# Tower of embedding, attention and product-key feed-forward on one core: key weights multiplied behind the embedding, and layer norm, scores and top-k of the product-key stage begun in the tail of the first attention

## The chip, the cores and the metric

One core of one Trainium2 chip runs the whole program. The metric is the device time of one execution in microseconds (us), lower is better. The core has a matrix engine (TensorE, PE in the profile; its weight loads are PEld), VectorE (DVE), ScalarE (ACT), GpSimd (POOL) and SyncE (SP), which here only issues DMA transfers. Each engine executes its own list of instructions in order, and the lists meet at semaphores.

## The reference

What is computed, cut to the stages (z is layer-normalised h; B = 4 sequences, S = 512 tokens, D = 128):

```python
h = event_table[x] + value_table[itok] + mask * (tanh(num * w1 + b1) @ w2 + b2)
h = h + attention0(layernorm(h))          # 8 heads of 16, distance-corrected logits
# product-key feed-forward on z = layernorm(h):
q = (z @ Wq + bq).reshape(-1, 8, 128)     # 8 heads
s1 = einsum('bhc,hnc->bhn', q[..., :64], keys[:, 0])   # 64 scores
s2 = einsum('bhc,hnc->bhn', q[..., 64:], keys[:, 1])   # 64 scores
s1t, i1 = top_k(s1, 8);  s2t, i2 = top_k(s2, 8)
scores, best = top_k(s1t[..., :, None] + s2t[..., None, :], 8)
idx = i1 * 64 + i2 at best
vals = relu(z . w_down[idx]) * softmax(scores)
h = h + vals @ w_up[idx]
h = h + attention1(layernorm(h))          # 8 heads of 64
h = h + experts(layernorm(h))             # 16 experts, top-k tokens per expert
```

## The kernel before

The residual stream `h` stays in on-chip memory for the whole program as 16 tiles of 128 tokens; a batch is one sequence of 4 tiles. The stages follow each other, and each engine's part is written out by hand in one function per engine (`sync`, `gpsimd`, `scalar`, `vector`, `tensor`), so the order of the work is the order of the lines.

**Start.** SyncE issues 16 small and middle loads. GpSimd issues 32 indirect gathers of table rows (L346), eight per batch: batches 0 and 1, then the reciprocal root of the first layer norm (`rstd_step`, L356), then batches 2 and 3, then a power for the first attention (L374). TensorE makes the numeric part of the embedding of all four batches (L1141), VectorE adds it up (`embed`), makes the statistics of batch 0 (`ln_stats`, L689 to L694) and normalises (`ln_scale`, L701). `heads0` then makes queries, keys and values.

**First attention.** `attention(a0, b)` runs 32 units (8 heads x 4 tiles) through all engines: logits on TensorE, maximum on VectorE (L717), exponential on ScalarE (L463), division on GpSimd (L364), transposition on TensorE (L1097), split copies on ScalarE (L472) and VectorE (`expT_lo`, L730), product with the values on TensorE (`pv`, L1109), which runs eight steps behind the logits. For batches 0 to 2 the call is given `next_ln`: VectorE puts the statistics of the next batch behind unit 28's `expT_lo` (s == UNITS) and the scaling behind unit 30's, and TensorE transposes the result at s == UNITS + 3. For batch 3 nothing is given. `project0` (L1132, L1133) waits for the copy of the last product (L477) and writes bank 6; `residual` (L747) adds it to `h`.

**Product keys.** After that residual SyncE loads `pk_wqT` and `pk_keys` (512 KB each) into `vals_t`; VectorE spreads the bias (L853); TensorE folds query weights and keys into one matrix, `keyw`, and the bias into `keyb` (L1198, four groups of four products, each product two passes); ScalarE and VectorE copy them out (L534, L538, L946). Then come `ln_stats(lnC, 0)` on VectorE, `rstd_step` and `normalise_xn(0)` (L423) on GpSimd. From there tile t goes: `scores(t)` on TensorE (transpose L1210, products L1218 and L1219, the latter with `ones_r` and `keyb`), copy to `sc` on ScalarE (L548), `half_max` (L858), `half_index` (L865), `pair_scores` (L870), `pair_best` (L876 to L883) and `expert_numbers` (from L890) on VectorE, `expert_numbers` on GpSimd (L401 to L414), `transpose_uvp` on TensorE (L1226), then `one_hots` on VectorE (from L918) and `spread`. `expert_numbers` on VectorE waits at L893 for the exponential of the pair scores. ScalarE makes that exponential (`softmax_exp(0)`, L572) behind `copy_scores(1)`, the eight pieces of `relu_inner(0)` (L557) and `expand_indices(0)` (L566), and TensorE makes the products for those eight pieces (`inner(0)`, L1237) behind `scores(1)`. Tiles 0 and 1 are prepared in this way ahead of the loop over the 16 tiles; in the loop tile t + 2 is prepared beside tile t. TensorE's list at this place is:

```python
scores(0, 0)
scores(1, 0)
inner(0, 1)
transpose_uvp(0)
scores(2, 1)
transpose_uvp(1)
for t in range(NT):
    spread(t, 0, 2)
```

After the 16 tiles come the second attention and the experts, which the change doesn't touch.

Of the kernel before, what the change touches and what calls it, by code (L numbers as in the profile page):

```python
# [13 lines left out]
def tower(nc, x_idx, val_idx, num_rows, mask_idx, event_table, value_table, tok_w1, tok_b1, tok_w2b2,  # L14
# [7 lines left out]
    P = 128  # L22
# [5 lines left out]
    H = 8  # L28
# [19 lines left out]
    LOGITS = (0, 1, 6)  # L48
    GATED = 9

    with ExitStack() as ctx:
# [38 lines left out]
        wo0 = sb("wo0", [P, H // HPG, D])  # L90
        wqkv0 = sb("wqkv0", [P, 3 * D])
# [53 lines left out]
        k4 = qkv0[:, :, D:2 * D].rearrange("p j (h d) -> p j h d", h=H)  # L145
        qa = q_aug[:].rearrange("p (j h) a -> p j h a", j=TPB)
# [10 lines left out]
        w_v = sC.sb("w_v", [P, T2, 2, 2, NV, 2], F16)  # L157
        iota_u = sC.sb("iota_u", [P, NU, 2], F16)
        iota8 = sC.sb("iota8", [P, TOP, HK], F16)
        ident16 = sC.sb("ident16", [P, P], F16)  # L160
        wqT_s = vals_t[:, 0:1024].rearrange("p (h d) -> p h d", h=H)
        keys_s = vals_t[:, 1024:2048].rearrange("p (h n) -> p h n", h=H)
        bqb_s = vals_t[:, 2048:3072].rearrange("p (h t) -> p h t", h=H)
        keyw = sC.sb("keyw", [P, H * P])
        keyb = sC.sb("keyb", [P, H * P], F32R)
        ones_r = sC.sb("ones_r", [P, P], F32R)
# [4 lines left out]
        g_sb = sC.sb("g_sb", [P, 3, GT * NV])  # L171
# [120 lines left out]
        def _(sp):  # L292
# [15 lines left out]
            sp.dma_start(wo0[:], a0_wo.rearrange("p (g d) -> p g d", g=H // HPG)).then_inc(ld_a0, 16)  # L308
            sp.wait_ge(h_ready, B)
# [23 lines left out]
        def _(pool):  # L333
            nc.gpsimd.memset(ident[:], 0.0)
            nc.gpsimd.memset(ones[:], 1.0)
            nc.gpsimd.memset(mhalf[:], -0.5)
            nc.gpsimd.memset(phalf[:], 0.5)
# [44 lines left out]
            pool.wait_ge(a0.add, B)  # L382
# [5 lines left out]
            nc.gpsimd.memset(psp[:], 0.0)  # L388
            nc.gpsimd.memset(ones_r[:].bitcast(F32), 1.0).then_inc(consts, 1)
# [37 lines left out]
            rstd_step(lnC, 0, TPB)  # L427
            normalise_xn(0)
# [19 lines left out]
        def _(act):  # L448
# [5 lines left out]
            def attention(a, b, next_ln=None):  # L454
# [24 lines left out]
                for s in range(UNITS + 9):  # L479
# [7 lines left out]
                    if s == UNITS + 4 and next_ln is not None:  # L487
                        copy_xnT(next_ln, b + 1)

# [33 lines left out]

            copy_xnT(lnB, 0)
# [4 lines left out]
            attention(a0, B - 1)  # L529


            for n in range(2):
                act.wait_ge(kw_ps, n + 1)
                nc.scalar.copy(keyw[:, n * 512:(n + 1) * 512], bank[n][:, :]).then_inc(kw_sb, 1)  # L534
# [915 lines left out]
```

## Time and profile before

| | before |
|---|---|
| median of 3 runs | 1363.96 us (1362.43 to 1366.89) |
| the profiled execution | 1364.92 us, its span 1363.1 us |
| busy share of the span | PE 80%, PEld 61%, DVE 76%, ACT 51%, POOL 47% |
| granted TensorE clock over the span | 0.919 of full |
| DMA over the span | 14.63 MB, 11 GB/s on average |

The profile shows one execution; the span begins with its first instruction and ends with its last, and 1.82 us of its time lie outside. A share is an average over stages with different limits, so the stage around the change is read by itself below. "L1198" is line 1198 of the kernel before.

### The profile page before, as it was taken

The numbers are of one execution on the slowest core, as the hardware profiler recorded it, in microseconds if no ns is written. First come the engines' busy times: TensorE is split into PE (matmuls) and PEld (weight loads), VectorE is DVE, ScalarE is ACT, GpSimd is POOL, SyncE is SP. The second block draws the span as 40 slices with busy tenths as digits, with TensorE's granted clock in tenths as the row PEclk, the third lists the DMA queues.
The fourth block names the chain that finished last, engine by engine and source line by source line (L and its number), as shares of the span: only waits on it lengthen the run. The fifth ranks groups of instructions, "written<-read, shape, count | busy, mean of one in ns | idle before, by whom it ended". The sixth has DMA issues, their size and how long they took to land.

```text
span 1363.1 us, 24162 instructions
## 1 busy us (share of the span) xinstructions
PE 1091.6 (80%) x7848; PEld 835.8 (61%) x7848; DVE 1032.9 (76%) x2991; ACT 689.3 (51%) x1457; POOL 643.4 (47%) x530
## 2 busy tenths in 40 slices
PE   4386785867943888888888878789999898979997
PEld 2354554545532777777777778455665655656675
DVE  4697685976828999999999997387585876844587
ACT  1484674856713344344434433277484775815433
POOL 7474361743623776876677665154260542610000
PEclk9698897998977899898899989899899899978999
DMA  3300000000000000000000001100000000000000
GB/s 78 142 1 1 0 0 0 0 0 0 1 31 1 1 2 2 2 2 2 1 2 2 1 2 40 77 1 1 0 0 0 0 0 1 1 1 1 1 8 23
DMA packets 6425, 14.63 MB, mean 11 GB/s; under 512 B 1855, under 2 KB 4482, under 8 KB 5762
## 3 DMA queue, kind: packets, MB, share of 16 engines
q1 hardware_dynamic: 5314, 11.42, 2.4%
q0 software_dynamic: 1024, 2.10, 0.6%
q8 instruction: 49, 0.80, 0.3%
q14 instruction: 38, 0.31, 0.1%
HBM read 12.47 MB, written 1.05 MB: 10 GB/s over the span
## 4 chain that ended last, share of the span: by engine, by line
issue 32%; DVE 31%; PE 25%; POOL 6%; DVEq 3%; ACT 2%; POOLq 1%; DMA 0%; ACTq 0%; SPq 0%
DVE one_u L927 6%; DVE w_v L921 5%; PE quad L1349 4%; PE quad L1097 4%; PE bank L1344 4%; DVE a_eT L730 4%; DVE i L865 3%; PE quad L1109 3%; POOL wu L346 2%; DVE vals L936 2%; DVE m L858 2%; DVE bi L883 2%; POOL a_en L364 1%; DVEq L920 1%; DVE a_negmax L717 1%
## 5 line engine op out<-in xcount | busy, mean ns | idle before, releaser
L364 POOL TENSOR_TENSOR a_en<-a_e,a_rrec 128x512 f32<-128x512 f32 x256 | 265.1, 1040 | 300.7 <-DVE a_rrec L724 282.9
L717 DVE TENSOR_REDUCE a_negmax<-bank 128x1 f32<-128x512 f32 x256 | 176.1, 691 | 44.7 <-PE bank L1295 28.3
L463 ACT ACTIVATE a_e<-bank,a_negmax 128x512 f32<-128x512 f32 x256 | 176.3, 689 | 64.2 <-DVE a_negmax L717 53.6
L1097 PE MATMUL quad<-ident,a_en 128*128 128x128 f32 x1024 | 166.4, 287 | 42.1 <-DVE a_eT L730 35.2
L1097 PEld LDWEIGHTS quad<-ident,a_en 128*128 128x128 f32 x1024 | 112.4, 145 | 135.4 <-issue 121.7
L730 DVE TENSOR_TENSOR a_eT<-quad,a_eT 128x512 fp32r<-128x512 f32 x256 | 172.6, 676 | 4.5 <-ACT a_eT L472 4.3
L1109 PE MATMUL quad<-a_eT,a_v 128*128 128x512 f32 x512 | 174.1, 431 | 1.0 <-DVE a_eT L730 0.9
L396 POOL TENSOR_TENSOR vals<-relu_in,g_sb 128x512 f32<-128x512 f32 x80 | 141.3, 1792 | 40.4 <-ACT g_sb L590 21.3
L472 ACT CAST a_eT<-quad 128x512 fp32r<-128x512 f32 x256 | 148.0, 578 | 15.2 <-PE quad L1097 15.2
L1237 PE MATMUL bank<-xnT,wd 128*128 128x128 f32 x1024 | 129.0, 283 | 3.1 <-ACT relu_in L557 1.3
L1237 PEld LDWEIGHTS bank<-xnT,wd 128*128 128x128 f32 x1024 | 121.5, 195 | 8.8 <-ACT relu_in L557 8.4
L1268 PE MATMUL bank<-wu,vals 128*128 128x128 f32 x1024 | 119.3, 278 | 4.8 <-issue 4.8
L1268 PEld LDWEIGHTS bank<-wu,vals 128*128 128x128 f32 x1024 | 117.9, 195 | 4.9 <-issue 4.9
L1257 PE MATMUL quad<-w_v,one_u 128*128 128x64 f16 x2048 | 77.6, 199 | 46.5 <-DVE one_u L927 25.4
L1257 PEld LDWEIGHTS quad<-w_v,one_u 128*128 128x128 f16 x2048 | 71.0, 101 | 59.9 <-DVE one_u L927 35.0
L927 DVE TENSOR_TENSOR one_u<-iota_u,uv 128x2048 f16<-128x2048 f16 x64 | 97.4, 1580 | 0.0
L1295 PE MATMUL bank<-a_kT,a_qT 128*128 128x512 f32 x256 | 84.8, 419 | 9.3 <-DVE a_v L998 6.9
L557 ACT ACTIVATE relu_in<-bank 128x512 f32<-128x512 f32 x128 | 75.2, 596 | 24.1 <-PE bank L1237 22.4
L1349 PEld LDWEIGHTS quad<-wu,hidT 128*128 128x128 f32 x512 | 67.6, 194 | 31.4 <-issue 27.4
L1109 PEld LDWEIGHTS quad<-a_eT,a_v 128*128 128x128 f32 x512 | 79.6, 190 | 5.9 <-DVE a_eT L730 2.4
L590 ACT COPY g_sb<-quad 128x512 f32<-128x512 f32 x16 | 9.4, 587 | 138.9 <-PE quad L1257 138.9
L661 ACT ACTIVATE hidT<-bank,b1e 128x512 f32<-128x512 f32 x64 | 44.0, 687 | 62.7 <-PE bank L1344 62.4
(210 smaller groups left out, 2023.2 us busy)
## 6 DMA issues: line engine op xcount, KB each, us to landing
wd<-in_pk_down SPq DMA_DIRECT2D x1, 2048.0 KB, 8.3
wu<-in_pk_up SPq DMA_DIRECT2D x1, 2048.0 KB, 12.8
wu<-in_moe_w SPq DMA_DIRECT2D x2, 1024.0 KB
out<-h SPq DMA_DIRECT2D x4, 256.0 KB, 2.3
wd<-in_num_rows SPq DMA_DIRECT2D x1, 512.0 KB
vals<-in_pk_wqT SPq DMA_DIRECT2D x1, 512.0 KB, 3.7
vals<-in_pk_keys SPq DMA_DIRECT2D x1, 512.0 KB, 4.6
wd<-in_a_wq SPq DMA_DIRECT2D x1, 512.0 KB
```

The source lines that it names most:

```text
L364: nc.gpsimd.tensor_tensor(m.en[:, s % 3, :], m.e[:, s % 3, :], m.rrec[:, s % 4:s % 4 + 1].to_broadcast([P, S]), ALU.mult).then_inc(a.nr, 1)
L396: nc.gpsimd.tensor_tensor(*weigh_args(t, c, k, g_sb[:, slot, :])).then_inc(vals_pool, 1)
L463: nc.scalar.activation(m.e[:, s % 3, :], bank[LOGITS[s % 3]][:, :], ACT.Exp, bias=m.negmax[:, s % 4:s % 4 + 1], accum_out=m.rowsum[:, s % ...
L472: nc.scalar.copy(m.eT[:, hd % 2, 0, :, j * P:(j + 1) * P], bank[2 + s % 2].rearrange("p (c n) -> p c n", c=TPB)).then_inc(a.hi, 1)
L717: V.tensor_reduce(m.negmax[:, s % 4:s % 4 + 1], bank[LOGITS[s % 3]][:, :], AX.X, ALU.max, negate=True).then_inc(a.mx, 1)
L730: V.tensor_tensor(part[:, 1], bank[2 + s % 2].rearrange("p (c n) -> p c n", c=TPB), part[:, 0].bitcast(F32), ALU.subtract).then_inc(a.lo, 1)
L927: V.tensor_tensor(one_u[:, c * n:(c + 1) * n], iota_u[:].unsqueeze(1).to_broadcast([P, n, NU, 2]), token_pairs(uv[:, t % 2, 0, c * GT:(c + ...
L1097: last = tp(bank[2 + s % 2][:, c * P:(c + 1) * P], m.en[:, s % 3, c * P:(c + 1) * P], ident[:])
L1109: last = mm(bank[4 + g % 2], m.v[:, c, hd, :], m.eT[:, hd % 2, part, c, :], start=(hd % a.group == 0 and c == 0 and part == 0), stop=(hd % ...
L1237: last = mm(bank[g % 2][:, q * P:(q + 1) * P], wd[:, IG * g + q, :], xnT_tile(t), start=True, stop=True)
L1257: made = mm(quad[:, 2 * (c % 2) + i // half_pair, cols], one_u[:, pair // 2, :, pair % 2], w_v[:, pair // 2, k, :, :, pair % 2].rearrange( ...
L1268: last = mm(bank[6][:, 0:D], vals[:, v, :], wu[:, v, :], start=(v == 0), stop=(v == NV - 1))
```

## The change

The key weights are loaded, multiplied and copied in the start of the program, and the first tile of the product-key stage is normalised, scored and searched in the tail of the last batch's attention. In detail:

- SyncE: the loads of `pk_wqT` and `pk_keys` stand directly behind the load of `wo0` and go to the memory of `q_st`, which the first attention uses later. Before they waited for the last residual of the attention.
- `keyw`, `keyb` and `ones_r` get memory of their own; `ones_r` is filled in GpSimd's first instructions, `keyb` cleared in VectorE's first.
- TensorE multiplies the key weights behind the embedding products, into banks 1, 2, 3 and 7 (`KEY_BANKS`); it waits for the copies before it transposes the first normalised batch. ScalarE copies them before `copy_xnT(lnB, 0)`, VectorE does its part between `ln_stats` and `ln_scale` of batch 0.
- The last `attention(a0, B - 1)` is given `lnC` on VectorE, for batch 0 (tiles 0 to 3), and a `tail` on TensorE (transpose of tile 0 at s == UNITS + 3, its score products at UNITS + 5, ahead of the last two `pv` steps) and on ScalarE (copies at UNITS + 4 and UNITS + 6, ahead of the last `outT`).
- GpSimd no longer normalises batch 0 (`normalise_xn(0)` goes; VectorE does it) and makes its constants right behind `rstd_step(lnC, 0)`, without waiting for the residual.
- VectorE's residual of batch 3 moves behind the top-k search of tile 0, ahead of `expert_numbers(0)`. `scores(1)` and `inner(0)` stay behind `project0` on TensorE.
- `g_sb` and a placeholder `attention_tail` are laid out so that what the tail writes doesn't lie on memory which the attention still reads.

```diff
@@ sync
             sp.dma_start(wo0[:], a0_wo.rearrange("p (g d) -> p g d", g=H // HPG)).then_inc(ld_a0, 16)
+            sp.dma_start(wqT_s, pk_wqT.rearrange("p (h d) -> p h d", h=H)).then_inc(ld_pk, 16)
+            sp.dma_start(keys_s, pk_keys.rearrange("p (h d) -> p h d", h=H)).then_inc(ld_pk, 16)
             sp.wait_ge(h_ready, B)
...
-            sp.wait_ge(a0.add, B)
-            sp.dma_start(vals_t[:, 0:1024], pk_wqT).then_inc(ld_pk, 16)
-            sp.dma_start(vals_t[:, 1024:2048], pk_keys).then_inc(ld_pk, 16)
@@ gpsimd
+            nc.gpsimd.memset(ones_r[:].bitcast(F32), 1.0)
...
             normalise(a0, B - 1)
-            pool.wait_ge(a0.add, B)
+            rstd_step(lnC, 0, TPB)
...
-            nc.gpsimd.memset(psp[:], 0.0)
-            nc.gpsimd.memset(ones_r[:].bitcast(F32), 1.0).then_inc(consts, 1)
+            nc.gpsimd.memset(psp[:], 0.0).then_inc(consts, 1)
...
-            rstd_step(lnC, 0, TPB)
-            normalise_xn(0)
             expert_numbers(0)
@@ scalar
+            for n in range(2):
+                act.wait_ge(kw_ps, n + 1)
+                nc.scalar.copy(keyw[:, n * 512:(n + 1) * 512], bank[KEY_BANKS[n]][:, :]).then_inc(kw_sb, 1)
+            act.wait_ge(kb_zero, 1)
+            for n in range(2):
+                act.wait_ge(kw_ps, n + 3)
+                nc.scalar.copy(keyb[0:1, n * 512:(n + 1) * 512], bank[KEY_BANKS[2 + n]][0:1, :]).then_inc(kw_sb, 1)
             copy_xnT(lnB, 0)
...
+            def first_scores(s):
+                if s == UNITS + 4:
+                    copy_xnT_tile(0)
+                if s == UNITS + 6:
+                    copy_scores(0)
+
+            attention(a0, B - 1, tail=first_scores)
             copy_xnT_tile(1)
@@ vector
+            V.memset(keyb[:].bitcast(F32), 0.0).then_inc(kb_zero, 1)
...
-            layer_norm(lnB, 0, 0, TPB)
+            ln_stats(lnB, 0, TPB)
+            dve.wait_ge(ld_pk, 48)
+            V.tensor_copy(bqb_s, bq_s[:].unsqueeze(2).to_broadcast([P, H, P])).then_inc(bq_b, 1)
+            for n in range(2):
+                dve.wait_ge(kw_sb, n + 3)
+                cols = slice(n * 512, (n + 1) * 512)
+                V.tensor_tensor(keyb[32:33, cols], bank[KEY_BANKS[2 + n]][0:1, :], keyb[0:1, cols].bitcast(F32),
+                                ALU.subtract).then_inc(kb_lo, 1)
+            ln_scale(lnB, 0, 0, TPB)
...
-            attention(a0, B - 1)
-            residual(a0, B - 1)
-            dve.drain()
+            attention(a0, B - 1, lnC, 0)
...
-            ln_stats(lnC, 0, TPB)
             dve.wait_ge(consts, 2)
             for t in range(2):
                 half_max(t)
...
                 pair_best(t)
+                if t == 0:
+                    residual(a0, B - 1)
+                    dve.drain()
                 expert_numbers(t)
@@ tensor
+            pe.wait_ge(ld_pk, 48)
+            for k, lhs in enumerate((wqT_s, bqb_s)):
+                if k:
+                    pe.wait_ge(bq_b, 1)
+                for q in range(2):
+                    for n in range(H // 2):
+                        hd = q * (H // 2) + n
+                        last = mm(bank[KEY_BANKS[2 * k + q]][:, n * P:(n + 1) * P], lhs[:, hd, :], keys_s[:, hd, :],
+                                  start=True, stop=True)
+                    last.then_inc(kw_ps, 1)
             pe.wait_ge(consts, 1)
             pe.wait_ge(ld_a0, 64)
...
+            pe.wait_ge(kw_sb, 4)
+            pe.wait_ge(kb_lo, 2)
             transpose_xn(lnB, 0)
...
+            def first_scores(s):
+                if s == UNITS + 3:
+                    transpose_tile(0)
+                if s == UNITS + 5:
+                    pe.wait_ge(a0.ex, B * UNITS)
+                    score_products(0, 0)
+
+            attention(a0, B - 1, logits0, tail=first_scores)
+            project0(B - 1)
+            pe.wait_ge(consts, 2)
+            pe.wait_ge(ld_exp, 32)
...
-            scores(0, 0)
             scores(1, 0)
             inner(0, 1)
```

## Rows read from the trace of the kernel before

**Rows 1.** Busy time by stretch: length, then PE, PEld, DVE, ACT, POOL; PEclk, DMA.

```profile
366.00:380.00 14.00, 11.56 (x61) 7.95 (x59) 5.35 (x10) 4.74 (x10) 3.08 (x3) 1.00 0.01 2
380.00:393.00 13.00, 5.20 (x32) 5.01 (x32) 3.62 (x8) 2.32 (x4) 2.97 (x5) 0.74 0.24 81
393.00:402.00 9.00, 0.45 (x1) 0.18 (x1) 0.89 (x7) 0.23 (x1) 4.16 (x5) 0.65 0.00 0
408.00:424.00 16.00, 9.04 (x69) 8.09 (x67) 12.92 (x94) 7.13 (x13) 3.01 (x7) 0.86 0.00 0
```

**Rows 2.** Timeline, attention's tail to first search: start, duration, engine, line [idle before <-releaser].

```profile
368.56 1.46 DVE L730 TENSOR_TENSOR a_eT<-quad,a_eT 128x512 fp32r<-128x512 f32 x2 [0.31 <-ACT a_eT L472]
...
372.33 2.11 PE L1109 MATMUL quad<-a_eT,a_v 128*128 128x512 f32 x8 [0.47 <-DVE a_eT L730]
374.47 0.59 ACT L477 COPY oT<-quad 128x512 f32<-128x512 f32 x1 [2.92 <-PE quad L1109]
...
379.44 0.69 DVE L747 TENSOR_TENSOR h<-h,bank 128x512 f32<-128x512 f32 x1 [7.16 <-PE bank L1133]
...
385.16 0.69 DVE L853 COPY vals<-bq_s 128x1024 f32<-128x1024 f32 x1 [5.04 <-DMA vals<-in_pk_keys]
...
385.91 3.41 PE L1198 MATMUL bank<-vals 128*128 128x128 f32 x16 [6.51 <-DVE vals L853]
...
389.16 1.95 PE L1198 MATMUL quad<-vals 128*128 128x128 f32 x16
...
391.75 0.68 DVE L946 TENSOR_TENSOR keyb<-quad,keyb 1x512 fp32r<-1x512 f32 x1 [0.16 <-ACT keyb L538]
...
398.00 3.14 POOL L423 TENSOR_SCALAR xn<-h,mv,rstd 128x128 f32<-128x128 f32 x4 [2.85 <-issue]
...
407.10 2.00 DVE L858 MAX8 m<-sc 128x8 f32<-128x64 f32 x15 [13.06 <-ACT sc L548]
```

**Rows 3.** Timeline, tail of batch 0's attention, with the next layer norm inside.

```profile
111.66 0.69 DVE L730 TENSOR_TENSOR a_eT<-quad,a_eT 128x512 fp32r<-128x512 f32 x1 [0.31 <-ACT a_eT L472]
...
114.95 1.12 DVE L701 TENSOR_SCALAR xn<-h,mv,rstd 128x128 f32 x4
...
116.12 0.66 PE L1084 MATMUL bank<-ident,xn 128*128 128x128 f32 x4
...
116.72 2.12 PE L1109 MATMUL quad<-a_eT,a_v 128*128 128x512 f32 x8
```

**Rows 4.** Timeline, scores of a later tile at the full clock.

```profile
474.06 0.31 PE L1210 MATMUL bank<-ident,xn 128*128 128x128 f32 x1
...
475.06 1.13 PE L1218 MATMUL bank<-keyw,xnT 128*128 128x512 f32 x2 [0.70 <-ACT xnT L451]
...
477.55 0.59 ACT L548 COPY sc<-bank 128x512 f32<-128x512 f32 x1 [0.45 <-PE bank L1219]
```

**Rows 5.** Timeline, inner products of tile 0 to the first one-hots.

```profile
409.51 7.53 PE L1237 MATMUL bank<-xnT,wd 128*128 128x128 f32 x64
...
418.88 0.22 DVE L893 TENSOR_REDUCE pz<-pe_ 128x8 f32<-128x64 f32 x1 [2.41 <-ACT pe_ L572]
...
435.60 1.21 DVE L918 TENSOR_TENSOR one_v<-iota_u,uv 128x2048 f16<-128x2048 f16 x1
```

**Rows 6.** Timeline of the start.

```profile
7.93 0.43 SPq L308 DMA_DIRECT2D wo<-in_a_wo  x1
...
15.95 1.91 PE L1141 MATMUL bank<-w2b,wd 65*128 65x128 f32 x8
...
23.52 1.06 POOL L356 TENSOR_TENSOR rstd<-veps,mhalf 128x4 f32<-128x4 f32 x1
...
51.84 0.18 DVE L817 TENSOR_SCALAR st<-st 128x32 f32<-128x32 f32 x1 [3.00 <-POOL st L374]
```

**Rows 7.** DMA issues: KB and us from issue to landing.

```profile
vals<-in_pk_keys SPq DMA_DIRECT2D x1, 512.0 KB, 4.6
```

**Rows 8.** Line L346, gathers of one table: ns min/median/max, first and last start us.

```profile
L346 POOL DMA_INDIRECT wu<-in_event_table,idx_e x16: 940/946/2162, 3.4 to 42.4; - x16
```

More of the change, by code:

```diff
@@ L48, in tower @@
     LOGITS = (0, 1, 6)
+    KEY_BANKS = (1, 2, 3, 7)
     GATED = 9
@@ L90, in tower @@
         wo0 = sb("wo0", [P, H // HPG, D])
+        keyw = sb("keyw", [P, H * P])
+        keyb = sb("keyb", [P, H * P], F32R)
+        ones_r = sb("ones_r", [P, P], F32R)
         wqkv0 = sb("wqkv0", [P, 3 * D])
@@ L145, in tower @@
         k4 = qkv0[:, :, D:2 * D].rearrange("p j (h d) -> p j h d", h=H)
+        key_load = q_st[:].rearrange("p n q a -> p (n q a)")
+        wqT_s, keys_s, bqb_s = [key_load[:, n * 1024:(n + 1) * 1024].rearrange("p (h d) -> p h d", h=H) for n in range(3)]
         qa = q_aug[:].rearrange("p (j h) a -> p j h a", j=TPB)
@@ L452, in copy_xnT, with attention @@
                                bank[7][:, 0:n]).then_inc(ln.sb, 1)
-            def attention(a, b, next_ln=None):
+            def attention(a, b, next_ln=None, tail=None):
                 m = a.mem
@@ L488, in attention @@
                         copy_xnT(next_ln, b + 1)
+                    if tail is not None:
+                        tail(s)
             act.wait_ge(ld_tok, 80)
@@ L528, in _ @@
                 heads0(b + 1)
-            attention(a0, B - 1)
-            for n in range(2):
-                act.wait_ge(kw_ps, n + 1)
-                nc.scalar.copy(keyw[:, n * 512:(n + 1) * 512], bank[n][:, :]).then_inc(kw_sb, 1)
-            act.wait_ge(kb_zero, 1)
-            for n in range(2):
-                act.wait_ge(kw_ps, n + 3)
-                nc.scalar.copy(keyb[0:1, n * 512:(n + 1) * 512], bank[2 + n][0:1, :]).then_inc(kw_sb, 1)
             def copy_xnT_tile(t):
@@ L708, in layer_norm, with attention @@
                 ln_scale(ln, i, first, n)
-            def attention(a, b, next_ln=None):
+            def attention(a, b, next_ln=None, n=None):
                 m = a.mem
+                n = b + 1 if n is None else n
                 def rowmax(s):
@@ L1085, in transpose_xn, with attention @@
                 last.then_inc(ln.ps, 1)
-            def attention(a, b, logits, next_ln=None):
+            def attention(a, b, logits, next_ln=None, tail=None):
                 m = a.mem
@@ L1124, in attention @@
                         transpose_xn(next_ln, b + 1)
+                    if tail is not None:
+                        tail(s)
             def project(a, b, wo, bo):
@@ L1187, in _, with transpose_tile @@
                 heads0(b + 1, b)
-            attention(a0, B - 1, logits0)
-            project0(B - 1)
-            pe.wait_ge(bq_b, 1)
-            pe.wait_ge(ld_pk, 48)
-            for k, lhs in enumerate((wqT_s, bqb_s)):
-                for q in range(2):
-                    for n in range(H // 2):
-                        hd = q * (H // 2) + n
-                        last = mm(bank[2 * k + q][:, n * P:(n + 1) * P], lhs[:, hd, :], keys_s[:, hd, :],
-                                  start=True, stop=True)
-                    last.then_inc(kw_ps, 1)
-            pe.wait_ge(kw_sb, 4)
-            pe.wait_ge(kb_lo, 2)
-            pe.wait_ge(consts, 2)
-            pe.wait_ge(ld_exp, 32)
-            def scores(t, inner_done):
+            def transpose_tile(t):
                 pe.wait_ge(lnC.xn, t // TPB + 1)
```

28 lines of the change are left out of this document (8 added, 20 removed).

## The prediction

> **What bounds the kernel now.** I read the page's busy slices first. The profile has no one bounding engine: PE is busiest over the span, yet around the 11th and 12th of 40 slices every engine's digit falls. I cut that place into stretches [rows 1]. From 366 to 380 the attention's tail is busy. From 380 to 402, 22 us, PE works 5.65 us, DVE 4.51, ACT 2.55, POOL 7.13: all wait for each other in turn. From 408 on DVE is busy 12.92 of 16 us. The timeline gives the order [rows 2]: last residual at 379.44, spreading of the bias at 385.16 (after 5.04 us of waiting for the key load), key products to 391.1, VectorE's last part of `keyb` to 392.43, normalising by GpSimd at 398.00, first search at 407.10. The waits agree: VectorE's 13.06 us before the search is the longest there, 5.04 and 7.16 are its others. So this stretch is a chain of hand-overs, and the reader is to see that DVE had finished the attention's last part at about 372.3 and could search only 35 us later. The next milestone is the start of `one_hots(0)` at 435.60 [rows 5], from which the regular tile loop runs.
>
> **The tail, step by step.** The layer norm in an attention's tail has its own rows: batches 0 to 2 do it already. In batch 0 the last eight value products begin 116.72 - 111.66 = 5.06 us after unit 28's `expT_lo` [rows 3]; in batch 3, without it, 372.33 - 368.56 = 3.77 us [rows 2]. The cost is 1.29 us. I carry rows 3 over by 368.56 - 111.66 = 256.90 us. Then `xn` is ready at 372.97 (114.95 + 1.12), PE transposes tile 0 at 373.02, ACT copies it by about 373.8 (copy of 128 columns, no wait before it), and the last `pv` steps begin at 373.62. Four steps were 2.11 us, so the two ahead of the scores take 1.06: score products begin at 374.7. A later tile at the full clock needs 2.45 us on PE, from 475.06 to just before the copy at 477.55, and 3.08 to the end of that copy [rows 4]. PE is free at 377.2, `sc` complete at 377.8, the last two `pv` steps end at 378.2. POOL's constants are 2.97 us of work [rows 1]; behind the reciprocal root, about 371.8, they are ready by 374.8 and hold nobody. So the search of tile 0 begins at 377.8 in place of 407.10: **29.3 us earlier**.
>
> That is not yet the gain. The copy for the projection comes at 378.3 in place of 374.47, 3.8 us later, because it stands behind score products and score copies. Projection to residual was 379.44 - 374.47 = 4.97 us, so `project0` ends at 383.2. Only then does PE begin `scores(1)`: transpose to first product 1.0 us [rows 4], 2.45 for the products, and `inner(0)` begins at 383.3 + 1.0 + 2.3 = 386.6. Its matmuls began at 409.51 before [rows 5]: **22.9 us earlier**. From its start to the reduction at 418.88 it was 9.37 us, through eight ACT pieces, the index expansion and the exponential in ACT's order; the reduction is now at 396.0.
>
> VectorE from search to that wait was 418.88 - 2.41 - 407.10 = 9.37 us. Begun at 377.8 it ends at 387.2; the residual (0.69 us, its projection done four us before) goes in between, to 388. VectorE then waits 8 us where it waited 2.41. The last 6.4 us of the 29.3 are thus lost to this wait, and behind it the order is unchanged to the one-hots: 435.60 - 22.9 = 412.7. The sum of the middle is -22.9. The removed load wait (5.04), key products (5.2), statistics and normalising on the path (14.7 from 392.43 to 407.10) are all contained in it and not counted again.
>
> **One pause that may move.** POOL's first `xn` instruction in the stage begins 2.85 us late, with "issue" as the reason [rows 2]: nothing the profile shows holds it. Before the change it is POOL's first TENSOR_SCALAR. That instruction goes, and the first TENSOR_SCALAR is then `jhi` in `expert_numbers(0)`. If the pause belongs to the first use it moves there, onto the path through `transpose_uvp(0)`, `copy_uvpT(0)` and `scores(2)` to the exponential of tile 1, which VectorE already waits for. If it belongs to that place or that form, it disappears or hides in a wait. The cost lies between 0 and 2.85; I take 2.85, since the only row of such a pause stands at a first use and DMA shows no traffic in that stretch [rows 1] that a reload of instructions would need. The Trainium skill, "GPSIMD Engine Reference", section Instruction dispatch, says that the first call of a freshly loaded kernel pays about 6 us with no visible instruction; no run here shows a load of that kind, and by that figure the sum would be an estimated -17, which stands outside my terms.
>
> **The start.** Every moved piece has a cover. SP issues two loads more behind `wo0` [rows 6], about 8.4 and 8.9; the wait behind them in its queue is for `h_ready`, much later. The larger landed 4.6 us after issue [rows 7], about 13.5; with the start's own transfers I allow 16. PE's embedding products end at 17.86 [rows 6], so it starts the key products then. They, with copies and `keyb`, took 385.91 to 392.43, and 1.46 less with both groups of 16 at the later 1.95 in place of 3.41 [rows 2]: 5.1 us, to 23.0. VectorE's scaling waits for POOL's root, which ends at 24.58 [rows 6], so 1.6 us stay free. Past that there is a second cover: DVE waits 3.00 us for POOL's power at 51.84 [rows 6]. Late by less than 4.6 us costs nothing. VectorE's `keyb` clearing and GpSimd's `ones_r` lie in the waits for the index load and the first embedding product. What is left uncovered is POOL, whose gathers and power are what DVE waits for at 51.84. The bias copy, 0.69 us [rows 2], now runs beside the gathers. Their median is 0.946 us and the longest 2.162 [rows 8], so one can overrun by 1.2: between 0 and 1.2 us, of which I take 0, the median being 6 ns over the shortest although VectorE works beside many of them. By the Trainium skill, "SBUF — State Buffer", section SBUF: two separate sides, a VectorE copy of fp32 between on-chip tiles locks GpSimd out of writing gather descriptors. By it the sum would be an estimated 0.7 less gain, by my row none.
>
> **The sum.** -22.9 + 2.85 + 0 = -20.0. The profiled execution has a span of 1363.1 and a time of 1364.92, 0.96 above the median. Its new span is 1343.1, its time 1344.9, and against the median it is 1344.
>
> **Rivals.**
> *The pause is not on the path.* All else holds: -22.9, 1341. For it: one row alone carries the pause, and the moved instruction reads its two factors from memory while `jhi` compares with a constant, so the first uses differ.
> *TensorE runs at the lower level.* In [rows 1] the clock falls to 0.65 after PE's long wait, while the tail before it has 1.00, the 2.4 GHz level. If the new stretch from 375 falls, `scores(1)` and `inner(0)` cost more: 16 products were 3.41 in place of 1.95, so 64 cost 5.8 more and the scores at most 1.9: 7.7 us, 1349 without the pause, 1351 with it. Against it: PE's waits there are about one us each. The Trainium skill, "TensorE: Matmul & The Clock Gate", Part 1, has the same two levels, the lower after idling; the trace agrees.
> *Slower: the loads land late.* VectorE waits for `ld_pk` between statistics and scaling, with `heads0` and then the whole program behind it, and PE does so before its first transpose. The cover ends at a landing of 24.6 + 3.0 - 5.1 = 22.5 us, and each us beyond costs one. The change loses from about 22.5 + 20 = 42.5 on. At 45 it gives 1366. The 4.6 us [rows 7] speak against it.
> *No change.* The exponential or PE's order could be bound by something that keeps its time, such as the expert weights; they were loaded long before, near 50 us. It gives 1364.
> *More.* If ACT or PE didn't hold the exponential, all 29.3 us would count: 1335. The order of their lists speaks against it.
>
> **How the numbers follow.** 45% for -20.0 (1344), 33% for -22.9 (1341), 9% for the lower clock (1349 to 1351), 7% for costs of one to four us that I don't see, 3% for more, 2% no change, 1% slower. The range 1338.5 to 1349 holds the first two with 2.5 us below for unmeasured gains at the joints and the lower clock's nearer end. A change under 0.3%, 4 us, can't be told from none. Faster 0.97, same 0.02, slower 0.01.
>
> **What would show it.** Right: key products near 18 to 22 us and DVE's scaling still near 24.6; attention's last eight value products split by score products; first search near 378; a VectorE wait near 8 us for the exponential, ended near 396; one-hots at 413 to 416. The pause shows as about 2.85 us in front of the first `jhi`. Wrong: `heads0` later than before, a search much after 378, a granted clock below 0.9 from 375 to 394, or a gap in the tile loop that was not there.

## The result and the profile after

The changed kernel takes 1345.56 us, the median of four runs from 1343.59 to 1352.04, where the kernel before takes 1363.21 beside it; the ratio is 0.9869, 95% interval 0.9834 to 0.9905. Timed once more it took 1343.86 (1341.74 to 1350.23) against 1365.82, a ratio of 0.9839 (0.981 to 0.9868). The forecast was 1344.0, a ratio of 0.9854, within 1338.5 to 1349.

The profiled execution took 1343.59 with a span of 1341.8. The first view of it is the busy time by stretch, in the stretches of [rows 1] (length, PE, PEld, DVE, ACT, POOL, PEclk, DMA share, GB/s):

```profile
366.00:380.00 14.00, 10.70 (x49) 6.93 (x50) 9.30 (x45) 4.22 (x8) 5.23 (x7) 1.00 0.01 2
380.00:393.00 13.00, 12.64 (x76) 9.90 (x76) 6.61 (x52) 5.02 (x9) 0.00 (x0) 0.87 0.00 0
393.00:402.00 9.00, 1.03 (x9) 0.84 (x8) 5.67 (x34) 2.38 (x5) 1.76 (x5) 0.70 0.00 1
408.00:424.00 16.00, 2.51 (x5) 0.88 (x3) 11.46 (x15) 2.37 (x5) 9.61 (x7) 0.61 0.00 0
```

The hole of 22 us is gone: from 380 to 393 PE works 12.64 of 13 us, where it had 5.20. What is left of the hole is VectorE's, as the timeline shows (start, duration, engine, line, idle before and its releaser):

```profile
366.47 0.69 DVE L732 TENSOR_TENSOR a_eT<-quad,a_eT 128x512 fp32r<-128x512 f32 x1 [0.31 <-ACT a_eT L470]
...
369.69 1.53 POOL L384 IOTA iota_u<- 128x256 f16 x1
...
369.76 2.24 DVE L702 TENSOR_SCALAR xn<-h,mv,rstd 128x128 f32<-128x128 f32 x4
...
373.69 1.02 PE L1217 MATMUL bank<-keyw,xnT 128*128 128x512 f32 x2
...
376.76 2.12 DVE L863 MAX8 m<-sc 128x8 f32<-128x64 f32 x16 [4.16 <-ACT sc L544]
377.00 0.59 ACT L475 COPY oT<-quad 128x512 f32<-128x512 f32 x1 [0.34 <-PE quad L1110]
...
385.88 0.69 DVE L749 TENSOR_TENSOR h<-h,bank 128x512 f32<-128x512 f32 x1
386.50 7.53 PE L1252 MATMUL bank<-xnT,wd 128*128 128x128 f32 x64
...
395.88 0.22 DVE L898 TENSOR_REDUCE pz<-pe_ 128x8 f32<-128x64 f32 x1 [8.96 <-ACT pe_ L568]
...
400.75 0.29 POOL L406 CAST uvp<-p 128x128 f16<-128x128 f32 x1 [2.78 <-issue]
...
415.52 1.21 DVE L923 TENSOR_TENSOR one_v<-iota_u,uv 128x2048 f16<-128x2048 f16 x1
```

Read it against [rows 2] and [rows 5]. The score products stand between two groups of value products, and the search begins at 376.76. VectorE comes through its search and the residual and then waits 8.96 us for the exponential, which hangs on the 64 inner products that PE began at 386.50. GpSimd's pause stands at 400.75, before a CAST.

Absolute times mix in what happened earlier, so from here on the stage is measured from the start of unit 28's second `expT` step on VectorE (368.56 before, 366.47 after):

| us behind that step | before | after | gained | forecast |
|---|---|---|---|---|
| first search | 38.54 | 10.29 | 28.25 | 29.3 |
| inner products of tile 0 | 40.95 | 20.03 | 20.9 | 22.9 |
| reduction of the exponentials | 50.32 | 29.41 | 20.9 | 22.9 |
| first one-hots | 67.04 | 49.05 | 18.0 | 20.0 |

Of the 21.3 us between the two spans the stage gave 18.0. The step itself came 2.1 us earlier, and the part behind the one-hots took 926.3 in place of 927.5 us. Neither is the change's: another profile of the kernel before, below, has its step at 366.69 and 926.3 us behind its one-hots.

The start, in the timeline of the changed kernel, answers to [rows 6]:

```profile
8.55 0.43 SPq L310 DMA_DIRECT2D q_st<-in_pk_wqT  x1
9.02 0.43 SPq L311 DMA_DIRECT2D q_st<-in_pk_keys  x1
...
17.52 0.69 DVE L771 TENSOR_TENSOR wu<-wu 128x512 f32<-128x512 f32 x1 [3.97 <-DMA wu<-in_value_table,idx_v]
...
17.73 1.91 PE L1154 MATMUL bank<-q_st 128*128 128x128 f32 x8
...
23.99 0.68 DVE L851 TENSOR_TENSOR keyb<-bank,keyb 1x512 fp32r<-1x512 f32 x1 [0.15 <-ACT keyb L530]
24.98 1.20 DVE L702 TENSOR_SCALAR xn<-h,mv,rstd 128x128 f32<-128x128 f32 x4 [0.31 <-POOL rstd L357]
...
51.80 0.18 DVE L820 TENSOR_SCALAR st<-st 128x32 f32<-128x32 f32 x1 [2.51 <-POOL st L375]
```

And the DMA issues, where [rows 7] had 4.6 us for the keys:

```profile
q_st<-in_pk_wqT SPq DMA_DIRECT2D x1, 512.0 KB, 6.3
q_st<-in_pk_keys SPq DMA_DIRECT2D x1, 512.0 KB, 8.1
```

The keys land at 9.02 + 8.1 = 17.1 us, just ahead of PE's first key product at 17.73, and they held up something else: VectorE's wait for the gathered rows ends at 17.52, where it ended at 14.99 before. The key work ends with VectorE's `keyb` at 24.67, GpSimd's reciprocal root at 24.95, so 0.31 us of cover were left. The step behind GpSimd's power stands at 51.80, as before (51.84).

### The profile page after: what moved, and what is told of

Same layout as the page of the kernel before. It is cut to its first block, busy times and chain, and to the rows that moved or that the text cites. A ratio compares the mean times of both kernels' runs of the same rounds, so it can differ in the third digit from the quotient of the medians.

```text
span 1341.8 us, 24161 instructions
## 1 busy us (share of the span) xinstructions
PE 1083.1 (81%) x7848; PEld 828.2 (62%) x7848; DVE 1037.9 (77%) x2995; ACT 689.5 (51%) x1457; POOL 640.7 (48%) x526
## 4 chain that ended last, share of the span: by engine, by line
DVE 35%; issue 32%; PE 20%; POOL 6%; DVEq 4%; ACT 2%; POOLq 0%; DMA 0%; ACTq 0%; SPq 0%
DVE one_u L932 7%; DVE w_v L926 5%; DVE a_eT L732 4%; PE quad L1098 4%; DVE i L870 3%; PE quad L1363 3%; PE quad L1110 3%; PE bank L1358 3%; POOL wu L347 2%; DVE vals L941 2%; DVE m L863 2%; DVE bi L888 2%; POOL a_en L365 2%; DVE a_negmax L719 1%; DVEq L925 1%
## 5 line engine op out<-in xcount | busy, mean ns | idle before, releaser
L1309 PE MATMUL bank<-a_kT,a_qT 128*128 128x512 f32 x256 | 81.2, 403 | 9.6 <-DVE a_v L999 6.9
```

## The experiments

Labels are those of the runs. "The step" is unit 28's second `expT` step, "the distance" is from it to the first one-hots.

**Where GpSimd's pause comes from.** Theory A: from the place in the instruction stream. Theory B: from the first drain behind the attention, wherever that stands.

```
             nc.gpsimd.memset(psp[:], 0.0).then_inc(consts, 1)
+            for _ in range(24):
+                nc.gpsimd.engine_nop()
```

> The changed kernel with 24 empty instructions on GpSimd behind its last constant. The 2.8 us pause in front of the cast in expert_numbers(0) is the 123rd or 124th instruction row of GpSimd's list in both kernels. Theory A, the pause belongs to a place in the instruction stream: it moves into the empty instructions, where GpSimd is idle for 24 us, the gap before the cast falls from 2.8 to 0.2 us, and the one-hots of tile 0 come 2.8 us nearer to unit 28's split copy (46.2 us in place of 49.05). Theory B, the pause belongs to the first drain after the attention: nothing changes, 2.8 us and 49.05. Theory C, of the prediction, first use of an instruction type: already contradicted, since the cast had been used before.

```
             nc.gpsimd.memset(psp[:], 0.0).then_inc(consts, 1)
+            pool.drain()
```

> The changed kernel with one drain on GpSimd behind its last constant. Theory B (the first drain after the attention pays): the pause goes there and the gap before the cast falls to 0.2 us, distance to the one-hots 46.2. Theory A (a place in the stream): one instruction more shifts the place by one, so a pause of about 2.8 us stays within an instruction or two of the cast and the distance stays near 49.

GpSimd's timeline with the no-ops:

```profile
422.38 0.29 POOL L408 CAST uvp<-p 128x128 f16<-128x128 f32 x1 [2.79 <-issue]
...
423.21 0.39 POOL L412 TENSOR_SCALAR jhi<-ij 128x64 f16<-128x64 f16 x1
```

and with the drain:

```profile
425.05 0.34 POOL L407 CAST uvp<-p 128x128 f16<-128x128 f32 x1 [0.15 <-issue]
...
426.13 0.39 POOL L411 TENSOR_SCALAR jhi<-ij 128x64 f16<-128x64 f16 x1 [0.17 <-DVE ij L917]
```

Twenty-four instructions more don't move the pause, one drain in GpSimd's idle time takes it away. Theory B holds. In the code a drain stands ahead of the CAST, and before the change the first drain behind the attention stood ahead of `xn`, where [rows 2] have the pause. Why a first drain costs this is not shown, nor is the place to which it went, since a drain has no row of its own. In the whole, e1_nops took 1365.74 and e2_drain 1368.2, far above the changed kernel, for another reason: all four variants timed on this chip, e1 to e4, reached the attention some 22 us late (below). And the distance with the drain was 49.4, with the no-ops 46.6, the wrong way round: VectorE's wait for the exponential was 11.77 us in one and 7.27 in the other. That asked for a look at TensorE's clock, which comes with e8.

**How the gain divides.** The key weights at the start, and the tail left as it was, with GpSimd normalising (ScalarE's and VectorE's lists go back in the same way):

```
-            rstd_step(lnC, 0, TPB)
+            pool.wait_ge(a0.add, B)
...
+            rstd_step(lnC, 0, TPB)
+            normalise_xn(0)
...
-            attention(a0, B - 1, logits0, tail=first_scores)
+            attention(a0, B - 1, logits0)
...
+            scores(0, 0)
```

> Half of the change: key weights at the start as in the changed kernel, but layer norm, scores and search of the product-key stage behind the residual as before, with GpSimd normalising. My theory that the stage is a chain: from the residual to the statistics nothing is left between, 12.3 us less (before: 393.4 less 0.9 against 380.2), so the first search comes 38.54 - 12.3 = 26.2 us behind unit 28's split copy and the one-hots at 67.04 - 12.3 = 54.7 us. Then 12.3 of the stage's 18.0 us come from the key weights and 5.7 from the tail. Rival: the weights' loads and products were hidden in part behind the other waits, distance over 58 us.

The step at 390.71, the search at 418.41, 27.7 us behind it, the one-hots at 447.05, a distance of 56.34. Of the 18.0 us, 67.04 - 56.34 = 10.7 come from the key weights and 7.3 from the tail (9.7 where TensorE keeps its full clock, below). Expected were 12.3 and 5.7, with the search at 26.2 and the one-hots at 54.7. Of the 1.5 us that the search came later than that, the trace explains 1.2: GpSimd's constants now stood on the path, and its reciprocal root began at 405.16, 2.86 us behind the residual, where before it began 1.70 us behind `keyb`. The pause of 2.85 us was back before `xn`. In the whole this half of the change took 1377.47, beside 1375.01 for the kernel before on that chip, each timed once: there the late start took more than the key weights gave.

**How much cover the start has.** VectorE held for 3.5 us between its part of the key weights and the layer norm of batch 0:

```
+            V.memset(mB.eT[:, 0].bitcast(F32), 0.0)
```

> The changed kernel with a clearing of 4096 columns (3.5 us, of memory that is written later anyway) on VectorE between the key part and ln_scale of batch 0. The covers measured in the changed kernel's profile are 0.31 us before the scaling and 2.51 us before VectorE's step behind GpSimd's power. If these are the covers, the step behind the power comes 0.7 us later than 51.80, at about 52.5. If the start has no cover, it comes 3.5 us later, at 55.3.

The step came at 394.15, 3.4 to 4.4 us later than in the three runs beside it (389.76, 390.59, 390.71). But in all four the start was late already, bound by the very hand-overs ahead of the memset, so this says nothing of the cover on an undisturbed start. In the whole it took 1370.29. It was run again as e8.

**Is the late start the change's?** The kernels themselves, on one more chip:

> The changed kernel unaltered, timed in three rounds against the kernel before, and profiled. The runs with the 24 no-ops, the drain and the delayed start all came from one chip, and all of them reached the batch loop some 24 us late, because the key products dribbled out of TensorE between 23 and 30 us and ScalarE copied them at 34 and 47 us. Theory 1 (the late start belongs to the chip or the execution, and the change is not its cause): the changed kernel shows the same late start where the chip has it, and the kernel before has it too, so that the ratio stays at 0.985 to 0.988. Theory 2 (the late start comes from the key loads and products, which put work of TensorE and ScalarE behind the gathers): the kernel before is free of it, and the ratio is near 0.9995 where the start is late, since 24 us of start take away more than the 21 us. On a chip where the first copy of the key weights stands at 20 us and VectorE's step behind GpSimd's power at 52 us, both say 0.987 and the question stays with the other runs.

> The kernel before, profiled on the same chip as the run of the changed kernel beside it. Theory 1 (chip or execution): VectorE's step behind GpSimd's power stands as late here as in the changed kernel, near 76 us where the start is late and 52 us where it is not. Theory 2 (the key work at the start): it stands at 52 us here whatever the changed kernel shows.

Neither kernel had the late start: the step behind the power stood at 51.84 and 52.04 us. The ratio of 0.9839 is told above. The question stayed open until e11. These two profiles gave something else. The distance was 51.98 in the changed kernel (49.05 in its first profile) and 69.34 in the kernel before (67.04), and where it grew the clock was down. Windows of e5_after_again:

```profile
376.00:382.00 6.00, 5.33 (x23) 3.37 (x21) 2.43 (x20) 1.76 (x3) 0.00 (x0) 1.00 0.00 0
382.00:392.00 10.00, 9.64 (x26) 6.01 (x25) 7.34 (x58) 1.24 (x3) 0.00 (x0) 0.53 0.00 0
```

**Three edits together.** The drain; GpSimd's iotas, and its other constants with them, held until VectorE has normalised tiles 0 to 3; and inner products before the projection:

```
             rstd_step(lnC, 0, TPB)
+            pool.wait_ge(lnC.xn, 1)
             nc.gpsimd.iota(iota_u[:], [[1, NU], [0, 2]], base=0, channel_multiplier=0,
...
             nc.gpsimd.memset(psp[:], 0.0).then_inc(consts, 1)
+            pool.drain()
...
-                if t == 0:
-                    residual(a0, B - 1)
-                    dve.drain()
                 expert_numbers(t)
+            residual(a0, B - 1)
+            dve.drain()
...
-            project0(B - 1)
...
             inner(0, 1)
+            project0(B - 1)
             transpose_uvp(0)
```

> The changed kernel with three edits: GpSimd drains once behind its last constant, it waits for VectorE's normalisation of tile 0 before it writes the two iotas, and TensorE does tile 1's scores and tile 0's inner products ahead of batch 3's output projection (VectorE's residual moves behind tile 1's expert numbers). Each has a place to show. The iotas: if GpSimd's writes beside it doubled the normalisation, its four operations take 1.12 us together again instead of 2.24, and the first search starts 1.1 us sooner, near 9.2 us behind the start of unit 28's second step (10.29 in the changed kernel); if the layer norm's operations are slow for another reason, they stay at 2.2. The order on TensorE: inner products of tile 0 start some 4 us earlier relative to that unit, near 15.5 to 16 us (20.0), if VectorE's wait at the reduction of the exponentials hung on them alone; it then falls from 9 to near 5 us. The drain: no pause of 2.8 us at GpSimd's cast. Together the one-hots start 41.5 to 43.5 us behind that unit (49.05), and the whole is 5 to 7.5 us faster than the changed kernel, a ratio to the kernel before near 0.982. Rival: the residual, moved from VectorE's idle time, and TensorE's projection, now behind the inner products, hold up something else (tile 1's layer norm is computed from the residual only for the last tiles, but scores of tile 2 wait for it), so that half of it is given back: 0.985.

1334.97 us (1333.46 to 1336.66), a ratio to the kernel before of 0.9775 (0.9748 to 0.9803), against 0.9839 for the changed kernel on the same chip. All three show at their places, in the timeline of e7_best:

```profile
369.51 0.69 DVE L734 TENSOR_TENSOR a_eT<-quad,a_eT 128x512 fp32r<-128x512 f32 x1 [0.31 <-ACT a_eT L472]
...
372.81 1.12 DVE L704 TENSOR_SCALAR xn<-h,mv,rstd 128x128 f32<-128x128 f32 x4
...
378.68 2.13 DVE L865 MAX8 m<-sc 128x8 f32<-128x64 f32 x16 [4.15 <-ACT sc L546]
...
382.01 7.53 PE L1252 MATMUL bank<-xnT,wd 128*128 128x128 f32 x64
...
391.39 0.22 DVE L900 TENSOR_REDUCE pz<-pe_ 128x8 f32<-128x64 f32 x1 [3.31 <-ACT pe_ L570]
...
393.64 0.34 POOL L408 CAST uvp<-p 128x128 f16<-128x128 f32 x1 [0.15 <-issue]
...
409.36 1.23 DVE L925 TENSOR_TENSOR one_v<-iota_u,uv 128x2048 f16<-128x2048 f16 x1
```

The normalisation takes 1.12 us for four operations, 2.24 with an iota beside it; the search comes 9.17 us behind the step (10.29); the inner products 12.5 us behind it (20.03), earlier than the 15.5 to 16 expected; the wait is 3.31 us, where 5 was expected; the distance is 39.85, better than the 41.5 to 43.5 expected. The rival, that half is given back, falls. But the granted clock stayed at the full level here until the inner products had ended, which it hadn't in the changed kernel's first profile, so part of the 9.2 us between 49.05 and 39.85 is not the edits' (the sum stands behind e9).

**The start's cover again, the order on TensorE alone, the drain alone:**

> The changed kernel with VectorE held 3.5 us (a memset of a buffer that is free there) between its part of the key weights and its layer norm of batch 0, run once more, since the first time the start was late for another reason. In the changed kernel VectorE waits 0.31 us for GpSimd at that layer norm and another 2.5 us (2.51, 2.47) at its step behind GpSimd's power at 51.8 us. Theory 1 (the layer norm of batch 0 sets the start once the 0.31 us are used up): the step behind the power moves from 51.8 to 55.0 us, and the whole takes some 3.2 us more than the changed kernel, a ratio to the kernel before near 0.987. Theory 2 (the 2.5 us at the later step are cover as well, because GpSimd gets there late for its own reasons, the gathers it issues): the step moves by 0.7 us at most and the ratio stays near 0.984.

> The changed kernel with one of the three edits of the fastest variant alone: tile 1's scores and tile 0's inner products ahead of batch 3's output projection. Theory 1 (VectorE's wait of 9 us at the reduction hangs on the inner products and with them on the projection ahead of them): the reduction stands 25 to 26 us behind unit 28's second step (29.4), the one-hots 44 to 45.5 us (49.05), and the whole is 3.5 to 5 us faster than the changed kernel, near 1339.5 us where the changed kernel takes 1344. Rival: GpSimd's pause of 2.8 us at its cast comes right behind the reduction, and the later residual adds 1.5 us to VectorE's path, so that 2 us are left.

> The changed kernel with the drain of GpSimd alone, timed in rounds. In its first run the pause was gone, but the lower clock of TensorE between 404 and 414 us hid what that gave. Theory 1 (the pause is on the path): one-hots 46 to 46.5 us behind unit 28's second step where TensorE's clock is that of the changed kernel (49.05), and the whole 2.8 us faster, near 1341. Rival (VectorE's wait for tile 1's exponential, 4.1 us, grows by what the pause gives back): the same time as the changed kernel; the first run had 1.5 us there, which speaks against it.

*e8* took 1346.45 us (1344.86 to 1347.61), ratio 0.9862 (0.9838 to 0.9885), and the step behind the power moved by 4.7 us, from 51.84 to 56.55, more than either theory said. GpSimd's timeline beside VectorE's memset (26.73 to 30.20), and the step itself, tell why:

```profile
25.52 1.02 POOL L347 DMA_INDIRECT wu<-in_event_table,idx_e  x1 [0.18 <-issue]
26.84 4.25 POOL L347 DMA_INDIRECT wu<-in_value_table,idx_v  x1 [0.30 <-issue]
31.40 0.95 POOL L347 DMA_INDIRECT wu<-in_event_table,idx_e  x1 [0.30 <-issue]
...
50.49 6.02 POOL L375 TENSOR_TENSOR st<-st,phalf 128x32 f32<-128x32 f32 x1
...
56.55 0.18 DVE L820 TENSOR_SCALAR st<-st 128x32 f32<-128x32 f32 x1 [3.05 <-POOL st L375]
```

One gather took 4.25 us in place of 0.95, so the delay was put on GpSimd's chain as well, and the run isn't the clean test that it was meant to be. The rows still tell which chain the step followed. GpSimd's power began right behind its last gather, and VectorE waited 3.05 us for it, so the 4.7 us came down GpSimd's list: 3.3 from this gather, 0.55 from the power (6.02 in place of 5.47), the rest from smaller ones. VectorE's scaling began 5.1 us later than in the changed kernel (30.12 for 24.98), and still all its work ahead of the step was done at 56.55 - 3.05 = 53.5, an estimated 1.7 us behind 51.84. So some 3.4 us of its delay were cover, which is nearer to theory 2 than to theory 1.

Unit 28's step came at 372.08 us, 2.9 later than in e10 on the same chip (369.14), not 4.9. That difference says little: from the step behind the power to unit 28's it takes between 314.7 and 317.6 us in the fourteen profiles, with no order by kernel.

The Trainium skill, "SBUF — State Buffer", section SBUF: two separate sides, has VectorE's two-port operations and GpSimd hold a shared port pair in turn, each for a whole instruction; reading the scaling as such an operation, the iota beside it agrees. In the changed kernel's profile the first of the four scalings, begun 0.07 us behind the iota, took 1.54 us and ended 0.08 us behind the iota's end, and the other three took 0.7 together. The stretched gather is less plain. At the start of the same profile a memset of the same size ran beside gathers that took their usual time:

```profile
7.12 3.47 DVE L756 MEMSET a_v<- 128x4096 f32 x1 [0.80 <-issue]
...
8.74 0.95 POOL L347 DMA_INDIRECT wu<-in_event_table,idx_e  x1 [0.30 <-issue]
```

So a memset alone doesn't hold a gather. What differs at 26.73 is that the scaling follows directly; whether that is the reason no run shows.

The profile of e8 was useful for its clock. Its windows from 379 to 395 lie at the same distance behind its step (372.08) as those of e5 above do behind theirs (369.20), and the level is full throughout:

```profile
379.00:385.00 6.00, 5.33 (x23) 3.32 (x22) 2.56 (x21) 1.76 (x3) 0.00 (x0) 1.00 0.01 3
385.00:395.00 10.00, 9.64 (x62) 7.81 (x62) 7.22 (x58) 3.83 (x7) 0.00 (x0) 1.00 0.00 0
```

In the same 9.64 us of busy PE, 62 matmuls were done here and 26 there; the count makes the difference look larger than it is, since the inner products, which are short, begin 18.34 us behind the step here and 22.17 there. With this the profiles of the changed kernel and its near relatives fall into three groups:

| profiles | clock while PE projects and scores tile 1 | wait for the exponential | distance |
|---|---|---|---|
| e8, e1, e4 | full level | 7.26 to 7.27 | 46.6 |
| the first profile | full, from about 383 to 386 the lower | 8.96 | 49.05 |
| e5; e10 and e2 (no pause) | lower level for about 10 us | 11.75 to 11.77 | 51.98; 49.4 |

*e9*, the order alone: 1338.62 us (1337.51 to 1340.01), ratio 0.9803 (0.978 to 0.9826). The reduction stands 23.0 us behind the step, where 25 to 26 was expected, and the distance is 43.33, where 44 to 45.5 was expected, 3.3 less than e8's at the same clock. The wait fell from 7.3 to 3.3, but from reduction to one-hots it took 20.33 in place of 18.88 us: of the 4.7 us by which the reduction came earlier 1.45 went back, as the rival said, not enough to leave 2 us only.

With e8 and e9 the 9.2 us between the changed kernel's first profile (49.05) and e7 (39.85) can be divided: 2.5 are the clock's (49.05 to e8's 46.59), 3.3 the order's (to e9's 43.33), and of the last 3.5 the scaling took 1.1 and the pause 2.4 by difference.

*e10*, the drain alone: 1343.7 us (1341.06 to 1346.78), ratio 0.9835 (0.9809 to 0.9862). The profile has the same clock as e5's in this stretch and a distance of 49.46 against 51.98: 2.5 us from the pause. The timing in rounds can't confirm that: 0.9835 against 0.9839 and 0.9869 for the changed kernel, each uncertain by 0.3%.

**The late start, on a chip that has it:**

> The kernel before, profiled once more. It bears on the late start only if this chip has it: in the first four runs, all on one chip, ScalarE's first copies of the key weights came at 34 and 47 us instead of 20 and 21, and the kernel before took 1375.0 us there. Theory 1 (the chip or the execution): the step of VectorE behind GpSimd's power stands at 60 us or later here too. Theory 2 (the key work at the start brings it): it stands at 52 us here, whatever the kernel beside it shows. If both kernels reach it at 52 us, the question stays open.

> The fastest variant once more, on whichever chip it gets. If its gain of 0.64% over the changed kernel (1334.97 against 1343.86 us) came from the three edits, the ratio to the kernel before is 0.976 to 0.980 again and the one-hots start 39.5 to 40.5 us behind unit 28's second step. If the first time was a favourable spell of TensorE's clock, the ratio is near 0.983. If the start is late here, the whole is some 24 us longer.

This chip had it. The kernel before took 1373.13 us (1369.83 to 1375.87), the fastest variant 1356.2 (1355.01 to 1361.74), a ratio of 0.9896 (0.9864 to 0.9928) in place of 0.9775. Its distance was 39.78, as expected, so the difference lies in the start; the whole is 21 us longer than e7, where some 24 was expected. The kernel before, e11_before_third:

```profile
26.09 1.08 PE L1084 MATMUL bank<-ident,xn 128*128 128x128 f32 x4 [7.76 <-DVE xn L701]
...
33.23 0.58 ACT L451 COPY xnT<-bank 128x512 f32<-128x512 f32 x1 [22.20 <-remote]
...
40.93 0.56 DVE L782 TENSOR_TENSOR qkv<-quad,bqkv 128x384 f32<-128x384 f32 x1 [3.54 <-remote]
...
45.12 0.56 DVE L782 TENSOR_TENSOR qkv<-quad,bqkv 128x384 f32<-128x384 f32 x1 [3.63 <-remote]
...
60.60 0.18 DVE L817 TENSOR_SCALAR st<-st 128x32 f32<-128x32 f32 x1
```

The fastest variant, e12_best_again, on the same chip:

```profile
28.69 0.59 ACT L528 COPY keyw<-bank 128x512 f32<-128x512 f32 x1 [17.71 <-PE bank L1155]
33.65 0.59 ACT L528 COPY keyw<-quad 128x512 f32<-128x512 f32 x1 [4.38 <-remote]
38.67 0.57 ACT L532 CAST keyb<-quad 1x512 fp32r<-1x512 f32 x1 [4.43 <-remote]
48.41 0.57 ACT L532 CAST keyb<-bank 1x512 fp32r<-1x512 f32 x1 [9.16 <-remote]
...
72.83 0.18 DVE L822 TENSOR_SCALAR st<-st 128x32 f32<-128x32 f32 x1
```

Two readings. In both kernels hand-overs that take a fraction of a us elsewhere take 4 to 9 us here, from about 24 us on until a few us behind GpSimd's last gather, which is issued at 43.7 in e11 and at 44.1 in e12. "Remote" is a releaser that the profile can't name. So the late start belongs to the chip, as theory 1 says. But the kernel before has its statistics, scaling and transposes of batch 0 behind it by 27 us and meets the bad spell with a few hand-overs, while the changed kernels have first to pass the key products to ScalarE and `keyb` to VectorE, and batch 0's scaling stands behind these. The step behind the power comes at 60.60 in the one and at 72.83 in the other (74.25 with the no-ops on the first such chip), where it was 51.4 to 52.1 in both on other chips (e8, which was held back, apart). So theory 2 is right as well: by one profile of each, the change loses 12 us more than the kernel before there. On the first such chip e1_nops took 1365.74 and the kernel before, timed once, 1375.01: by that about 9 us of the gain are left, and e3, which has only the key weights, was 2.5 us slower than the kernel before. The changed kernel itself was never run on such a chip. What holds the hand-overs up while the gathers run is not shown by any view.

## Why the prediction was right

**The sum.** Forecast -20.0; the stage gave 18.0 in the profile, and the two timings 17.6 and 22.0 us between medians. The forecast lies between them, and where a timing falls is partly chance: the stage's own gain moves with TensorE's clock, as the groups above show. With the clock at its full level the gain would be 67.04 - 46.6 = 20.4.

**The tail.** The search came 28.25 us earlier, not 29.3. The step that was off is that POOL's constants "hold nobody": the first iota (369.69 to 371.22) ran beside VectorE's scaling and held the first of its four operations for 1.54 us (0.35 in e7), so that the four took 2.24 us in place of 1.12. e7, where the iotas wait, has it back at 1.12. The order on PE, the 8 us wait (8.96) and the landing of the projection behind the score products went as worked out.

**The inner products.** 20.9 us earlier, not 22.9. With the clock at its full level they begin 18.34 us behind the step (e8), so of the 20.03 here 1.7 come from the clock, which the windows show at 0.61 from 382 to 386. The 0.3 us that are left are the iota's 1.1 less what other steps came out shorter than worked out. This is the lower-clock rival, which the prediction held at 9% and priced at up to 7.7 us; it came, in part or in whole, in four of the seven profiles of the table above. Between its ends, in the changed kernel and its near relatives, the distance goes from 46.6 to 52.0, 5.4 us. The kernel before varies too: 66.81 (e11), 67.04 and 69.34. At the full clock the distance is 46.6 against a forecast of 415.6 - 368.56 = 47.0. The sentence "PE's waits there are about one us each", which was to speak against the rival, was right of the waits and didn't keep the clock up.

**The pause.** Its price was right, 2.78 for 2.85, and that it would stand on the path; its reason was wrong. It didn't go with the first TENSOR_SCALAR (`jhi` at 401.59 has none) but with the first drain behind the attention. That the term held is luck in this respect: the first drain happens to stand two instructions ahead of the one that was named. On the path the pause is worth 2.4 to 2.5 us (e7 against e9, e10 against e5). Without it the sum would have been 1341, the second case.

**The start.** Nothing was lost on undisturbed chips, as forecast, but the cover was thinner than the 1.6 us worked out: 0.31. The landing of the keys isn't the reason, since PE began its products at 17.73 and had been expected at 17.86. The step that was off is the price of the products: all 32 were taken at 1.95 us for 16, and the first 16 took about 3.5 (8 in 1.91), about the pace that they had at the lower level before. The granted clock reads 1.00 there, so the profile doesn't explain it. The products ended at 23.3 and `keyb` at 24.67. "Late by less than 4.6 us costs nothing" was not tested cleanly: e8 delayed GpSimd too, and its rows speak for a cover of some 3.4 us. The bias copy beside a gather made one of them 1.27 us long instead of 0.95 and cost nothing at 51.80.

**The slower rival.** It was put on the landing of the loads, which was never late enough. A late start came by another way, hand-overs during the gathers on two of the chips, and cost about 12 us. By e1 it would not have turned the sign, but it puts the ratio there at 1365.74 / 1375.01 = 0.993, each timed once, and that lies outside the range, whose upper end was 0.989. That the recorded timing fell on a chip without it is luck too.

## What to carry to other kernels

Work moved to the start is only free while its hand-overs are: an engine that first has to pass something on inherits every delay of the engines before it, and the chip at hand may not show it. A stage made denser isn't bound by the same thing in every execution: let TensorE do the longest chain first (here inner products before a projection that nobody waits for). Whether less depends on the clock then is not shown: on one chip, four runs each, the fastest variant took 1333.5 to 1336.7 us and the changed kernel 1341.7 to 1350.2, but on another the fastest variant took 1355.0 to 1361.7. And measure a stage from a mark inside it, not from the start of the span.

## What the runs showed of the hardware

- The first drain of GpSimd behind the first attention took 2.8 us more (2.85, 2.78, 2.79), put down to "issue"; a drain while the engine is idle takes it off the path (0.15 left).
- An iota of GpSimd, which only writes, held the first of VectorE's four scalings beside it for 1.54 us, to 0.08 us behind the iota's end. The other way round, GpSimd's `jhi` of tile 1 (L411, 416.94 in the changed kernel), which takes 0.43 us otherwise, took 4.59 beside a VectorE product of 4.43 (L926, from 416.81).
- A gather of GpSimd took 4.25 us beside a 3.47 us memset of VectorE with a scaling behind it, and 0.95 beside an equal memset at the start.
- TensorE's granted clock in the same stretch of the same program was 1.00 or 0.53, after the same work and the same gaps of about one us; no profile here tells when it will be which. In the variants that do the inner products first (e7, e9, e12) it stayed at 1.00 until those had ended, and the wait for the exponential was 3.31 us each time; whether the order keeps it there, three profiles can't tell.
- On two of the chips hand-overs between engines took some 4 to 12 us while the indirect gathers ran, and went back to normal behind them.
